# First attention of a two-layer block with folded weights, dispatch in halves, and low halves moved to VectorE

## The reference

```python
# x: (4, 512, 256)
qkv = xn @ w_qkv.T + b_qkv                    # one head of width 256
q, k, v = split(qkv, 3)
probs = softmax(q @ k.T / sqrt(256))          # within a batch
attention = (probs @ v) @ w_out.T + b_out

probs = softmax(xn @ gate_weight.T)           # 16 experts, the 4 largest of a token
routed = sum over the 4: prob * ((silu(xn @ w_gate[e]) * (xn @ w_up[e])) @ w_down[e])   # F = 176
shared = (silu(xn @ ws_gate) * (xn @ ws_up)) @ ws_down                                  # F = 352
x = x + attention + routed + shared
```

## Time and profile before

| | |
|---|---|
| median of 3 runs | 1144.38 us (1143.2 to 1147.49) |
| span of the profiled execution | 1136.1 us |
| what lies around the span in an execution | about 8 us: the median less the span |
| mean granted TensorE clock | 0.968 of full |
| TensorE busy | 1018.1 us, 90% |
| VectorE, ScalarE, GpSimd busy | 762.7, 604.8, 317.4 us |

### The profile page before, as it was taken

One profiled execution on the slowest core, in us unless ns is written; L12 is line 12 of the kernel. 1 busy time (PEld: TensorE's weight loads), 2 busy tenths in 40 slices (PEclk: granted clock), 3 DMA queues, 4 the chain that ended last, 5 costly groups with the idle time before them and its releaser, 6 DMA issues.

```text
span 1136.1 us, 17535 instructions
## 1 busy us (share of the span) xinstructions
PE 1018.1 (90%) x5780; PEld 743.6 (65%) x5780; DVE 762.7 (67%) x1591; ACT 604.8 (53%) x911; POOL 317.4 (28%) x331
## 2 busy tenths in 40 slices
PE   4998898779999846799999999999999997999995
PEld 3877776669999724555555555555555565888884
DVE  6576454556655346798899888888888846444437
ACT  6325445355565543466665666666666665444431
POOL 2005777066655500000000122222221000455441
PEclk9999999989999967899999999999999998999999
DMA  6863333354444272011111222222222124333253
GB/s 231 315 263 126 124 110 120 113 195 150 136 124 135 89 305 35 14 28 29 29 29 29 43 55 57 56 56 57 56 56 43 63 73 155 108 108 101 92 196 137
DMA packets 49140, 120.49 MB, mean 106 GB/s; under 512 B 7752, under 2 KB 24904, under 8 KB 48520
## 3 DMA queue, kind: packets, MB, share of 16 engines
q1 hardware_dynamic: 36096, 82.80, 25.5%
q0 software_dynamic: 11808, 32.37, 7.5%
q10 hardware_dynamic: 1152, 4.19, 0.9%
HBM read 72.30 MB, written 52.42 MB: 110 GB/s over the span
## 4 chain that ended last, share of the span: by engine, by line
PE 65%; DVE 16%; POOL 7%; issue 4%; ACT 3%; DMA 3%; SPq 0%; ACTq 0%; DVEq 0%; POOLq 0%
PE psum L817 11%; PE psum L838 9%; PE psum L826 7%; DVE work_f L1699 6%; POOL xg L466 5%; PE psum L633 5%; PE psum L634 4%; PE psum L635 4%; PE psum L547 3%; PE psum L548 3%; PE psum L549 3%; PE psum L619 3%; PE psum L644 2%; DVE x L1310 1%; PE psum L665 1%
## 5 line engine op out<-in xcount | busy, mean ns | idle before, releaser
L1699 DVE TENSOR_REDUCE work_f<-psum 128x1 f32<-128x512 f32 x512 | 337.3, 685 | 49.1 <-PE psum L817 46.7
L1203 ACT ACTIVATE work_f<-psum 128x1024 f32<-128x1024 f32 x172 | 169.5, 1023 | 104.9 <-PE psum L826 100.5
L817 PE MATMUL psum<-work_r 128*128 128x512 f32 x512 | 207.8, 445 | 18.9 <-DVE work_f L1699 7.0
L473 POOL DMA_INDIRECT yk<-yb,dest x134 | 131.3, 980 | 240.1 <-ACT yb L1057 206.7
L817 PEld LDWEIGHTS psum<-work_r 128*128 128x128 f32 x512 | 93.4, 190 | 133.8 <-DVE work_f L1699 71.2
L826 PE MATMUL psum<-qm,work_r 128*128 128x512 f32 x512 | 160.8, 396 | 0.9 <-ACT work_f L1203 0.8
L466 POOL DMA_INDIRECT xg<-xn,slot x112 | 108.2, 966 | 180.9 <-PE psum L853 143.5
L826 PEld LDWEIGHTS psum<-qm,work_r 128*128 128x128 f32 x512 | 93.8, 188 | 24.1 <-ACT work_f L1203 6.2
L633 PE MATMUL psum<-wexp,xbh 128*128 x268 | 102.1, 381 | 7.4 <-issue 7.2
L1203 ACT ACTIVATE pt<-psum 128x1024 f32<-128x1024 f32 x84 | 82.8, 1022 | 45.9 <-PE psum L826 42.7
L634 PE MATMUL psum<-wexp,xbh 128*128 x268 | 96.4, 360 | 0.0
(11 more groups left out here) (218 smaller groups left out, 2065.2 us busy)
## 6 DMA issues: line engine op xcount, KB each, us to landing
xb<-xg SPq DMA_DIRECT2D x67, 258.0 KB
xg<-in_pad SPq DMA_DIRECT2D x1, 10320.0 KB
yg<-yk SPq DMA_DIRECT2D x20, 512.0 KB, 9.0
stage<-in_moe SPq DMA_DIRECT2D x16, 608.0 KB
xg<-in_pad SPq DMA_DIRECT2D x1, 7224.0 KB
work_r<-work_r SPq DMA_DIRECT2D x128, 48.0 KB
work_r<-work_r SPq DMA_DIRECT2D x32, 192.0 KB
stage<-in_moe SPq DMA_DIRECT2D x16, 384.0 KB, 3.7
```

The lines of the kernel that those rows point to most:

```text
L473: nc.gpsimd.indirect_dma_start(yk[l], bass.IndirectOffsetOnAxis(ap=dest[:, j % 8, i:i + 1], axis=0), yb[l][:, j % 2, i, :], None).then_inc ...
L817: nc.tensor.matmul(next_bank(pe, ("scores", n), b_mx, n + 1), qs[g % 2][:, t * P:(t + 1) * P], km[g % 4][:, r, :], start=True, stop=True). ...
L1203: nc.scalar.activation(pt[((b * NG + g) * QT + t) % 3][:, 2 * h:2 * h + 2, :], psum[:, 3 + 2 * h:5 + 2 * h, :], ACT.Exp, scale=float(HD) * ...
L1699: v.reduce_max(mx[:, s % 2, i:i + 1], ring["scores", n], AX.X).then_inc(b_mx, 1)
```

## The change

**Folded weights.** With one head, the scores are `xn (Wq^T Wk) xn^T`, a term of `bq` per key, and a constant per query row, which shifts a row as a whole. The kernel now multiplies `Wq^T Wk` and `Wv^T Wo^T` on the chip once (`fold_weights`), with the biases' parts (`row_constants`, `bq_fold`, an addition to the output bias `bo`), and splits the results (`fold_high` on ScalarE, `fold_low` on VectorE, ahead of shared tile 2). A batch has two query slices and four value tiles to project instead of six slices and four output tiles; the keys are the normalised tokens themselves, and the values come out by token, already projected. `fold` carries a factor of -1/16, so row maxima are now minima and the exponential has scale -1. A small operation with the row's constant follows each minimum, where one with -1/16 did before.

**Order in a batch.** Exponentials are transposed unscaled, in two banks by turns instead of four, and the reciprocal sum is applied when the result is added to `x`, in four operations of 256 columns instead of one of 1024. There is no context and no copy of it.

**Dispatch.** `m_slot` is now signalled before the block numbers are made, which have their own `m_eid`. The two columns are written for halves of eight tiles, each with its own `m_scat[h]`, so a half waits for the same half of the choice before.

**Low halves.** Experts 0 to 4 move from GpSimd to VectorE, two experts to each batch's place between the last low half and the addition to `x`. High halves move in the same way. SyncE loads experts 0 to 9, the first when the fold has read the raw weights (`k_bias`, the buffers overlap), then waits for the dispatch.

The diff, cut:

```diff
-        BY_DVE = (5, 6, 7, 8, 10, 12, 14, 15)
+        BY_DVE = (0, 1, 2, 3, 4, 5, 6, 7, 8, 10, 12, 14, 15)
...
-            for e in range(8):
+            sp.wait_ge(k_bias, 1)
+            for e in range(10):
                 load_expert(e)
-            sp.wait_ge(m_scat, scattered(0, 16 * TT * TOP0))
+            for h in range(2):
+                sp.wait_ge(m_scat[h], scattered(0, 8 * TT * TOP0))
             load_pair(0, 0)
             load_pair(0, 1)
-            for e in range(8, 11):
-                load_expert(e)
-            more = {3: (11,), 4: (12,), 5: (13, 14), 6: (15,)}
+            load_expert(10)
+            more = {2: (11,), 3: (12,), 4: (13,), 5: (14,), 6: (15,)}
...
-                if t == 0:
+                if t % (TT // 2) == 0:
+                    of = slice(t, t + TT // 2)
                     if k:
-                        pool.wait_ge(m_scat, scattered(l, 16 * TT * k))
+                        pool.wait_ge(m_scat[t // (TT // 2)], scattered(l, 8 * TT * k))
...
-                    pool.wait_ge(m_dc, choices(l, k + 1))
...
+                    pool.wait_ge(m_dc, halves_of_choices(l, 2 * k + t // (TT // 2) + 1))
                 at = t * TOP[l] + k
                 nc.gpsimd.indirect_dma_start(xg[l], bass.IndirectOffsetOnAxis(ap=slot[l][:, at:at + 1], axis=0),
-                                             xn[l][:, t, :], None).then_inc(m_scat, 16)
+                                             xn[l][:, t, :], None).then_inc(m_scat[t // (TT // 2)], 16)
...
-            first_piece = {6: 0, 22: 1, 34: 2, 46: 3, 56: 4}
-            second_piece = {12: 0, 28: 1, 40: 2, 51: 3, 60: 4}
             for n in range(TT * TOP0):
-                if n in first_piece:
-                    low_down(first_piece[n])
-                if n in second_piece:
-                    low_rest(second_piece[n])
                 dispatch(0, n)
             low_expert(9)
...
+            def row_constants():
+
+                pe.wait_ge(s_raw, 16)
+                pe.wait_ge(k_prod, 1)
+                pe.wait_ge(s_xl, 2)
+                for k in range(KH):
+                    for c in range(KH):
+                        nc.tensor.matmul(psum[:, 1, k:k + 1], square(raw0, 0)[:, c, k * P:(k + 1) * P], bq0[:, 2 + c:3 + c],
+                                         start=c == 0, stop=c == KH - 1)
+                for c in range(KH):
+                    ins = nc.tensor.matmul(psum[:, 1, 4:5], ones, bqk_rows[:, c:c + 1], start=c == 0, stop=c == KH - 1)
+                ins.then_inc(k_row, 1)
+
+            def fold_weights():
+
+                pe.wait_ge(s_lc, 1)
+                for n, bank in ((0, 4), (2, 5)):
+                    hi, lo = ([square(raw_split[:, i, :], n + m) for m in range(2)] for i in range(2))
+                    for k in range(KH):
+                        for c in range(KH):
+                            col = slice(k * P, (k + 1) * P)
+                            ins = mm3(psum[:, bank, k * H:(k + 1) * H], hi[0][:, c, col], lo[0][:, c, col],
+                                      hi[1][:, c, :], lo[1][:, c, :], k == 0 and c == 0, k == KH - 1 and c == KH - 1)
+                    ins.then_inc(k_fold, 1)
+                for k in range(KH):
+                    for c in range(KH):
+                        nc.tensor.matmul(psum[:, 6, k:k + 1], square(raw0, 1)[:, c, k * P:(k + 1) * P], bq0[:, c:c + 1],
+                                         start=c == 0, stop=c == KH - 1)
+                pe.wait_ge(k_bv, 1)
+                for c in range(KH):
+                    ins = nc.tensor.matmul(psum[:, 6, H:2 * H], bv_rows[:, c, :], square(raw0, 3)[:, c, :],
+                                           start=c == 0, stop=c == KH - 1)
+                ins.then_inc(k_bias, 1)
...
+            def values0(b1, c):
+
+                for i in range(KH):
+                    for t in (0, 1):
+                        tok = slice(b1 * S + (2 * c + t) * P, b1 * S + (2 * c + t + 1) * P)
+                        ins = mm3(psum[:, 6 + c, t * H:(t + 1) * H], xt_hi[0][:, i, tok], xt_lo[0][:, i, tok],
+                                  vo_fold[0][:, i, :], vo_fold[1][:, i, :], i == 0 and t == 0, i == KH - 1 and t == 1)
+                ins.then_inc(a_vx, 1)
+
+            def exponents_t(b, t):
+                pe.wait_ge(a_e, b * QT + (t + 1))
+                if t >= 2:
+                    pe.wait_ge(a_pl, b * QT + (t - 1))
+                for c in range(QT):
+                    ins = nc.tensor.transpose(psum[:, 4 + t % 2, c * P:(c + 1) * P], prob[:, t, c * P:(c + 1) * P], ident)
+                ins.then_inc(a_pt, 1)
...
-                    project0(0, 4, b + 1, 4)
-
+                    queries0(b + 1, 6)
+                exponents_t(b, 0)
+                exponents_t(b, 1)
+                if not last:
+                    pe.wait_ge(a_lo, (b + 1) * KH + 1)
+                    values0(b + 1, 0)
+                exponents_t(b, 2)
+                exponents_t(b, 3)
+                if not last:
+                    pe.wait_ge(a_lo, (b + 2) * KH)
+                    values0(b + 1, 1)
...
+                        q = slice(t * P, (t + 1) * P)
+                        ins = mm3(o, p_hi[:, c, q], p_lo[:, c, q], v_hi[:, c, :], v_lo[:, c, :], c == 0, c == QT - 1)
+                    if t % 2:
+                        ins.then_inc(a_o, 1)
+
+            row_constants()
+            tokens_t(0, B - 1)
...
+            fold_weights()
...
+                v.memset(small[0:1, 79:80], 0.0).then_inc(m_slot, 1)
+                yield
...
-                                ALU.add, ALU.mult).then_inc(m_slot, 1)
-                dve.wait_ge(m_slot, layers(l, 1))
+                                ALU.add, ALU.mult).then_inc(m_eid, 1)
+                dve.wait_ge(m_eid, layers(l, 1))
...
+            def fold_low():
+                for n, by in ((0, -1.0 / 16.0), (1, 1.0)):
+                    dve.wait_ge(k_hi, n + 1)
+                    v.scalar_tensor_tensor(out=fold[:, n, 1].rearrange("p k h -> p (k h)"), in0=psum[:, 4 + n, :], scalar=by,
+                                           in1=fold[:, n, 0].rearrange("p k h -> p (k h)").bitcast(f32),
+                                           op0=ALU.mult, op1=ALU.subtract).then_inc(k_lo, 1)
+                dve.wait_ge(k_bias, 1)
+                v.tensor_scalar(bq_fold, psum[:, 6, 0:KH], -1.0 / 16.0, None, ALU.mult)
+                v.tensor_tensor(bo[0], bo[0], psum[:, 6, H:2 * H], ALU.add).then_inc(k_done, 1)
...
-
+                    row = row_const[:, b * QT + t:b * QT + t + 1]
+                    v.scalar_tensor_tensor(out=sm[:, 1, t:t + 1], in0=sm[:, 0, t:t + 1], scalar=row, in1=row,
+                                           op0=ALU.subtract, op1=ALU.add).then_inc(a_n, 1)
+                if b < B - 1:
+                    queries0(b + 1, 6)
+                dve.wait_ge(a_e, (b + 1) * QT)
+                v.reciprocal(sm[:, 3, :], sm[:, 2, :]).then_inc(a_r, 1)
...
+                for e in experts:
+                    low_expert(e)
+                dve.wait_ge(a_r, b + 1)
+                for t in range(QT):
+                    if t % 2 == 0:
+                        dve.wait_ge(a_o, b * 2 + (t // 2 + 1))
+                    tile = x[:, b * QT + t, :]
+                    ins = v.scalar_tensor_tensor(out=tile, in0=psum[:, 2 + t // 2, (t % 2) * H:(t % 2 + 1) * H],
+                                                 scalar=sm[:, 3, t:t + 1], in1=tile, op0=ALU.mult, op1=ALU.add)
+                ins.then_inc(a_y, 1)
+                if b < B - 1:
+                    values0(b + 1, 0)
+                    values0(b + 1, 1)
...
+            for b, experts in enumerate(((0, 1), (2, 3), (4, 5), (6, 7))):
+                attention0(b, experts)
+            low_expert(8)
```

320 lines of the change are left out of this document (151 added, 169 removed).

## The result

The changed kernel takes 1167.94 us (median of 4, 1166.22 to 1170.12) against 1143.79 for the kernel before (4, 1139.92 to 1147.49): ratio 1.0214, 95% interval 1.019 to 1.0239. I had forecast 1117. It is 2% slower, and 51 us from the forecast.

What follows compares the result with a forecast made beforehand. Two parallel chains, TensorE's attention and GpSimd's dispatch, were taken to bound the first attention, the dispatch after the change. -20.5 (first pair), -6 (head) and -0.6 (VectorE's last addition) gave -27 us: 1117 us, range 1106 to 1128.

Steps and rivals of the forecast that it cites:

- Ahead of the attention: Row constants (+1.6 us) and weight fold (+4.9) on TensorE end the shared stage 6.5 us later; first dispatch DMA at 96.3.
- The dispatch: GpSimd's 64 indirect DMAs, first issue to last, shrink from 100.4 to 87.1 us; last issue at 183.4 instead of 195.88.
- the 4.0 us of contention: Nine low parts on VectorE stretch GpSimd's DMAs during dispatch by 0.45 us each, 4.0 together; bounds 0 and 14.2.
- Out go five low parts of experts ... 13.9: Low parts leaving GpSimd's dispatch save 15.3 us of busy time, less ten reopened gaps: 13.9 us.
- Out go three waits ... 6.0: In GpSimd's dispatch, dropping three waits for all DMAs of a choice saves 6.0 us.
- Rival 4: Slower: TensorE idles so often that its clock stays at 1.2 GHz; attention ends at 240, time 1168 us; chance 0.02.
- The attention alone: First attention takes 19.2 us for each batch, 16 for the last, starting at 99.4 and ending at 173.
- What TensorE's chain alone would gain: In the first attention, shortening only TensorE's chain gains about 12 us, as it ends that long after the first pair's fetch.
- rival 6: The dispatch is not shortened (late fill, waiting halves); only TensorE's 12 us are gained, less the later start: 1133 us; chance 0.03.
- SyncE's order: Expert 9's load, waiting for low part 6 at about 170, precedes the first pair's fetch; dispatch hides it by 14 us.
- The head: Start of the routed stage, pairs 0 to 8: 12 us lost there, half given back, -6 us (bounds 0 and -10).
- The 8 us around the span: Time outside the profiled span of 1136.1 us, taken as about 8 and added to 1109 for the forecast of 1117.

Runs made afterwards that it cites:

- 3 x 2.7: Changed kernel with 3 idle breaks of 2.7 us on GpSimd, one after every 16 indirect DMAs of the dispatch: 1120.6 us, run again 1124.7 us.
- beside the shared experts: 3 x 2.7 plus 32 back-to-back indirect DMAs of 64 columns to an unread tensor, beside folded weights and shared experts: 1156.39 us.
- 7 x 2.7: Changed kernel with 7 idle breaks of 2.7 us on GpSimd, one after every 8 indirect DMAs of the dispatch: 1130.17 us, ratio 0.9895.
- short rows: Changed kernel with its dispatch moved behind the attention and 64 indirect DMAs of 64 of 258 columns, to an unread tensor, beside it: 1265.11 us.

## Why the prediction was wrong, point by point

**Ahead of the attention: right.** +6.5 forecast; the shared stage's last addition starts at 94.16 for 87.47, +6.7. The terms hold too: the first product of the logits starts at 25.21 for 23.52, +1.7 for 1.6, though the one-column products, of which no row had shown one, took 0.39 us each for 0.3 (eight records in 1.56 us for four products). First DMA 96.3 forecast, 96.16 measured.

**The dispatch: its own length right, its price wrong.** 87.1 us forecast, 84.4 measured. Without the 4.0 us of contention the forecast is 83.1, and VectorE, which makes it, stood still most of the time. With 3 x 2.7, where VectorE works beside it: 95.0 - 8.1 = 86.9. Of that 63 x 1.265 + 7 x 0.37 = 82.3 are issues and turns, so the low parts cost 4.6 for 4.0.

**The step that failed** is "Out go five low parts of experts ... 13.9. Out go three waits ... 6.0", together with "the end 99.4 + 57.6 + 16 = 173". I priced the removed pauses on GpSimd alone, as gain, and the attention as if GpSimd were not there. The runs showed that TensorE lived on them: idle operations in their place bring its attention back to 179.5, or with one between any two DMAs to 173.0. The pauses, taken away, ended the dispatch 15 us earlier (180.55 for 195.88) and left the attention 68 us behind what it takes alone (241.3 for 173.5). None of my rivals had this mechanism. There was a trace of it in the kernel before: "remote" as a cause of 3.6 us of idle time of VectorE, which I quoted and never asked about; that kernel's batches of 29.5 us were 26.15 alone.

**Rival 4 was right in its number only.** It said 240 and 1168, and 241.3 and 1167.9 came. But it had three batches at 37 us and the last at 30 for a low clock; in fact the first took 88 and the others 18.9, 18.9 and 15.6, and beside the shared experts the hold-up began at full clock. The agreement is a coincidence.

**The attention alone: right**, 18.9 for 19.2, 15.6 for 16 in the last batch, 173.5 for 173.

**What TensorE's chain alone would gain: mis-read.** "Gains about those 12" sets TensorE's end at 210.46 against the fetch's issue at 198.53. The pair is there only some 4 us later, by the prediction's own figure, so it was about 8, and rival 6 some 4 us too fast. The forecast itself doesn't use the 12.

**SyncE's order: the hazard was named, and came true.** "It would cost what it is late": low part 6 came late, the load of expert 9 held the pairs' fetch until 237.83, 52 us behind the 186.0 of the forecast, though the dispatch was long over. It cost 1.6 us of its own: the attention's last product starts at 240.07, and TensorE then waits 1.62 us for the pair.

**The head: over-sized.** -6 forecast. First to last pair: 171.1 before, 169.3 after, 167.8 with 3 x 2.7, 166.9 with 7 x 2.7: 2 to 4.

**The 8 us around the span** were wrong: the profiled execution of the changed kernel took 1167.62 us for a span of 1165.5, so 2. The span of 1136.1 that I started from was a short one; 56 later executions of that kernel had 1136.8 to 1147.3.

With the hold-up mostly gone the parts roughly add up: 3 x 2.7 had a profiled span of 1116.1, 20.0 under the kernel before, of which 14.2 at the first pair (196.24 for 210.46), 3.3 up to the last pair, and 2.4 behind it, where nothing had been forecast. The forecast was 27, and 8 of these went into breaks.

## To carry to other kernels

A pause of one engine can be what another one lives on. Before counting a removed operation or wait as gain, look at what the others do during the pauses that it makes, and at every "remote" and "issue" of a few microseconds on them. Where GpSimd issues many indirect DMAs beside TensorE's work, space them: here 0.12 us more per DMA, or a microsecond after every eight, turned 2% lost into 1.4 and 1.7% won. And when a rival's number comes out, check its mechanism all the same.

## What the runs showed of the hardware

- Indirect DMAs issued by GpSimd every 1.265 us hold up TensorE in both kinds of work tried, after some 12 of them: groups of matmuls 0.6 to 2.8 us apart in the changed kernel, single ones mostly 1.4 to 3.5 us apart with short rows. With 1.39 us between most starts, 1.52 on average, the attention takes no longer than with no dispatch (173.0 and 173.5). Rows of 64 columns do it as rows of 258.
- The held matmuls, or groups of them, start whole steps of 0.70 us apart (138.35, 141.15, 143.95, 146.75 with short rows: 4 steps each).
- VectorE and ScalarE, where they wait for TensorE, go on up to 36 us behind the record of the product, 30 us beside the shared experts, while signals from ScalarE to VectorE take under 0.1 us (a cast ending at 112.94, its reader starting at 112.98).
- The transfers themselves don't lag: issued last at 180.55, the dispatch's queue has no packet after 184.

What GpSimd's issuing shares with TensorE stays open. The Trainium skill, "Perfetto Trace Analysis" (DMA Instruction — SWDGE (GPSIMD)), says that GpSimd's cores write the descriptors and that such a row ends with the last descriptor, not with the data. The trace agrees: the last row ends at 181.51, packets follow until 184. If so, the 0.96 us end with the writing, which fits that bytes don't matter. The Trainium skill, "NOTIFIC — the notification-queue block" (7.1 Overflow: three behaviours, one of which stalls the engine), says that the block that records events can hold an engine back when it can't keep up. No run here shows that it does. But every execution timed here was recorded, so whether an unrecorded kernel is held up in the same way was not tried.
